# A decoder layer: the second half's self queries and keys carried through DRAM instead of being multiplied out again, and self attention entered with fewer waits

## The reference

```python
x = x + self_attn(layernorm(x))          # 16 heads of 8, causal, scale 1/sqrt(128)
    qvk = h @ Wqvk; scores = q.k per head; softmax; @ v; @ Wo
x = x + cross_attn(layernorm(x), ctx)    # 16 heads of 8, keys = ctx @ Wk + bk
    k = ctx @ Wk + bk; v = ctx @ Wv + bv; softmax(q.k * 8**-0.5) @ v; @ Wo + bo
x = x + experts(layernorm(x))            # top 2 of 8, relu(x @ W1 + b1) @ W2 + b2
```

## Time and profile before

| | us |
|---|---|
| median of 3 runs | 936.83 |
| profiled execution | 941.72 |
| its span | 940.0 |
| ScalarE busy, share of the span | 832.9, 89% |
| TensorE busy, share of the span | 865.0, 92% |
| VectorE busy, share of the span | 500.2, 53% |

### The profile page before, as it was taken

How to read it: one execution, slowest core, us unless ns; L and a number is a source line. 1 busy time by engine, 2 the same in 40 slices (tenths; PEclk the granted TensorE clock), 3 DMA queues, 4 the chain that set the end, 5 groups by cost and what they waited for, 6 DMA issues and landing times.

```text
span 940.0 us, 16020 instructions
## 1 busy us (share of the span) xinstructions
PE 865.0 (92%) x6269; PEld 273.5 (29%) x6269; DVE 500.2 (53%) x981; ACT 832.9 (89%) x694; POOL 47.5 (5%) x104
## 2 busy tenths in 40 slices
PE   6987898999889999998999998999999999999997
PEld 4562222222222222222222232222233222223543
DVE  4765653341278767867875217255635553654432
ACT  4667887999999999999999999999999999998432
POOL 4000000000000000000000004000000000001300
PEclk9996998999999999999999999999999999999999
DMA  4153003811121111121221113323123310102120
GB/s 150 71 220 66 1 1 84 271 38 39 37 37 35 35 37 38 34 55 28 46 48 38 37 35 99 82 59 57 57 60 60 57 58 23 46 23 77 36 101 14
DMA packets 24814, 56.16 MB, mean 60 GB/s; under 512 B 6986, under 2 KB 12084, under 8 KB 24476
## 3 DMA queue, kind: packets, MB, share of 16 engines
q1 hardware_dynamic: 21276, 44.18, 18.5%
q0 software_dynamic: 3456, 10.88, 3.7%
HBM read 37.59 MB, written 9.59 MB: 50 GB/s over the span
## 4 chain that ended last, share of the span: by engine, by line
PE 54%; ACT 28%; issue 13%; DVE 4%; DMA 1%; SPq 0%; ACTq 0%; DVEq 0%
ACT probs L890 28%; PE psum L1731 23%; PE psum L1695 12%; PE psum L2023 3%; PE psum L2031 3%; PE psum L1676 2%; PE psum L1550 1%; PE psum L1590 1%; PE psum L1968 1%; PE psum L1669 1%; PE psum L1594 1%; PE psum L1851 1%; DVE turned L1128 1%; PE psum L1961 1%; PE psum L1727 1%
## 5 line engine op out<-in xcount | busy, mean ns | idle before, releaser
L890 ACT ACTIVATE probs<-psum 128x1536 f32<-128x1536 f32 x562 | 765.5, 1527 | 32.1 <-PE psum L1695 16.4
L1731 PE MATMUL psum<-probs,v_ctx 128*9 128x512 f32 x3080 | 402.7, 595 | 2.9 <-DVE turned L1128 2.9
L1695 PE MATMUL psum<-q_all,k_ring 32*128 32x512 f32 (+1 forms) x1732 | 284.2, 491 | 51.3 <-ACT probs L890 46.1
L1695 PEld LDWEIGHTS psum<-q_all,k_ring 32*128 32x128 f32 x1732 | 109.8, 185 | 403.6 <-ACT probs L890 356.8
L1171 DVE TENSOR_SCALAR attnT<-psum 128x512 f32<-128x512 f32 x60 | 41.5, 692 | 127.7 <-PE psum L1669 125.9
L1731 PEld LDWEIGHTS psum<-probs,v_ctx 128*9 128x9 f32 x3080 | 45.9, 88 | 98.8 <-issue 93.0
L961 ACT ACTIVATE probs<-psum,b_sb 128x512 f32<-128x512 f32 x32 | 22.0, 687 | 34.0 <-PE psum L2023 33.4
L1128 DVE STREAM_TRANSPOSE turned<-psum 128x512 f32<-128x512 f32 x16 | 11.5, 717 | 75.2 <-PE psum L1727 57.1
L1731 PE MATMUL psum<-probs,v_self 128*9 128x512 f32 (+3 forms) x384 | 43.0, 549 | 2.1 <-DVE probs L1149 1.4
L1182 DVE SCALAR_TENSOR_TENSOR kparts_bc<-kparts_bc,attnT 128x512 f32<-128x512 f32 x60 | 41.5, 692 | 2.0
L1172 DVE SCALAR_TENSOR_TENSOR attnT<-attnT,psum 128x512 f32<-128x512 f32 x60 | 41.2, 687 | 2.0
(11 more groups left out here) (247 smaller groups left out, 631.2 us busy)
## 6 DMA issues: line engine op xcount, KB each, us to landing
k_ring<-kc_parts SPq DMA_DIRECT2D x256, 52.0 KB
k_ring<-kc_parts SPq DMA_DIRECT2D x256, 48.0 KB
kc_parts<-kparts_bc SPq DMA_DIRECT2D x8, 512.0 KB, 2.8
q_all<-w_region POOLq DMA_DIRECT2D x13, 256.0 KB, 2.6
q_all<-ctx_region POOLq DMA_DIRECT2D x13, 256.0 KB, 2.7
kc_parts<-probs SPq DMA_DIRECT2D x4, 512.0 KB, 3.0
w_region<-in_L_ffn_W SPq DMA_DIRECT2D x1, 2048.0 KB, 10.4
probs<-gate_rows SPq DMA_DIRECT2D x2, 1024.0 KB, 5.5
```

The lines of the kernel that those rows point to most:

```text
L890: act.activation(probs[:, slot:slot + w, :], psum[:, at:at + w, :], ACT.Exp, scale=SC[ph]).then_inc(L[ph]["exp_done"], 1)
L1695: mm = pe.matmul(into[:, col:col + n_q], keys, q_all[rows, g, hf * HALF + q0:hf * HALF + q0 + n_q], start=True, stop=True)
L1731: mm = pe.matmul(into[:, q0:q0 + w], v_all[:, h, t, :], probs[:, place(ph, at)[1], col:col + w], start=first, stop=last)
```

## The change

**Quads.** Only the first half of the rows still gets quad products: 8, for 4 quads times queries and keys. For the second half the plain queries and keys of `self_squares`, which are in PSUM anyway, are split by ScalarE (high) and VectorE (low) into `self_parts` (in `attnT` and `heads`, free so long). SyncE stores the four parts, 256 KB each, to DRAM behind chunk 1's store, and lays them on the quads' rows by 32 loads of 8 partitions x 4 quads x 512 columns: two behind each store of chunks 4 to 11, 16 behind the last one. TensorE waits for all 32 before group 13 (`SECOND_HALF`).

**Entry.** `kparts` is turned, so that the last chunk is not in `probs`; the banks of the context's keys change places (`kctx_bank`), so that banks 0 to 2 are free earlier. ScalarE and VectorE read the verdict inside the chunk loop; the four copies of the cross query weights are made in chunk 8 rather than behind chunk 12. TensorE scores group 0 before the last norms and before its waits for the last chunk. ScalarE's waits for the squares to be read and for the one ring buffer in `probs` now stand ahead of group 2. VectorE clears the sums' bank between its reductions rather than behind them.

The core of the diff:

```diff
+def kctx_bank(c):
+    return 3 - c % 2
...
-        kparts = [kparts_a, kparts_bc[:, 0], kparts_bc[:, 1]]
+        kparts = [kparts_bc[:, 0], kparts_a, kparts_bc[:, 1]]
+        self_parts = ((attnT[:, 0:HALF], attnT[:, HALF:2 * HALF]), [heads[:, n * HALF // 32:(n + 1) * HALF // 32, :, :]
+                                                                    .rearrange("p c g d -> p (c g d)") for n in range(2)])
...
+            def store_self_parts():
+                sp.wait_ge(s["qkquad_split"], 2)
+                for which in range(2):
+                    for part in range(PARTS):
+                        sp.dma_start(qk_dram[which, part], self_parts[which][part]).then_inc(s["qk_stored"], 16)
+            def load_self_quads(n):
+                which, r, j = n // 16, n // 4 % 4, n % 4
+                if n == 0:
+                    sp.wait_ge(s["qk_stored"], 16 * 2 * PARTS)
+                row, part = ROWS * r + HD * j, (j // 2 if which else j % 2)
+                sp.dma_start((q_all, k_self)[which][row:row + HD, :, HALF:2 * HALF].bitcast(F32),
+                             qk_dram[which, part].rearrange("(g r d) c -> r d g c", g=QUADS, r=LANES)[r])\
+                    .then_inc(s["qk_loaded"], 16)
+            loaded = 0
             for c in range(NCHUNK):
                 w = min(CHUNK * P, KV - c * CHUNK * P)
                 sp.wait_ge(s["kctx_split"], c + 1)
                 sp.dma_start(kc_dram.rearrange("i p c -> p i c")[:, :, c * CHUNK * P:c * CHUNK * P + w],
                              kparts[c % KRING][:, :, 0:w]).then_inc(s[f"kctx_stored{c % KRING}"], 16)
+                if c == 1:
+                    store_self_parts()
+                todo = 0 if c < 4 else SELF_LOADS if c < NCHUNK - 1 else 32
+                for n in range(loaded, min(loaded + todo, 32)):
+                    load_self_quads(n)
+                loaded += todo
             for n in range(KRING):
                 sp.wait_ge(s[f"kctx_stored{n}"], 16 * len(range(n, NCHUNK, KRING)))
...
                 here = slice(n // 2 * HALF, (n // 2 + 1) * HALF)
                 act.activation((sq_q, sq_k)[n % 2][:, here], bank(QK_BANKS[n]), ACT.Square).then_inc(s["sq_self"], 1)
+                if n >= 2:
+                    evac(self_parts[n % 2][0].bitcast(F32R), bank(QK_BANKS[n]), s["qkquad_high"])
             def ctx_transposed(c):
...
-            for m in range(4 * QUADS):
+            for m in range(2 * QUADS):
                 act.wait_ge(s["qkquad_ps"], m + 1)
                 if m >= 2:
-                    act.wait_ge(s["qkquad_split"], m - 1)
+                    act.wait_ge(s["qkquad_split"], 2 + m - 1)
                 evac(high[:, m % 2, :].bitcast(F32R), bank(QK_BANKS[m % 4]), s["qkquad_high"])
...
             for c in range(1, NCHUNK):
                 ctx_keys(c)
                 if c + 2 < NCHUNK:
                     ctx_transposed(c + 2)
-            act.wait_ge(s["wlate_loaded"], 16 * LATE)
-            quad_weights(2, wq_sb[:, :], [sign * QUERY_SCALE for sign in Q_SIGNS], s["wcross_quads"])
+                if c == 6:
+                    self_bounded = verdict_of(act, 0)
+                if c == 8:
+                    act.wait_ge(s["wlate_loaded"], 16 * LATE)
+                    quad_weights(2, wq_sb[:, :], [sign * QUERY_SCALE for sign in Q_SIGNS], s["wcross_quads"])
...
+            def squares_read():
+                act.wait_ge(s["norms_done"], 2)
+                act.wait_ge(s["kctx_stored1"], 16 * len(range(1, NCHUNK, KRING)))
...
             def exponentials(ph, begin, end):
...
                     held = before_in(ph, g, 3)
+                    if ph == 0 and g == 2:
+                        squares_read()
                     if held is not None:
                         act.wait_ge(L[ph]["pv_batches"], batches_through(ph, held))
                     act.activation(probs[:, slot:slot + w, :], psum[:, at:at + w, :], ACT.Exp,
...
                             ins.then_inc(G[ph]["turned"], 1)
-            for n in range(KRING):
-                act.wait_ge(s[f"kctx_stored{n}"], 16 * len(range(n, NCHUNK, KRING)))
-            choose(act, 0, lambda: exponentials(0, 0, n_groups(0)), lambda: general_exponentials(0))
+            def general_self():
+                squares_read()
+                general_exponentials(0)
+            act.cond(self_bounded, lambda: exponentials(0, 0, n_groups(0)), general_self)
             exponentials(1, 0, PART_AT)
...
-            for m in range(4 * QUADS):
-                g, which, hf = m // 4, m // 2 % 2, m % 2
-                dve.wait_ge(s["qkquad_high"], m + 1)
-                dst = (q_all, k_self)[which][:, g, hf * HALF:(hf + 1) * HALF]
+            for n in range(2, 4):
+                dve.wait_ge(s["qkquad_high"], n - 1)
+                step(dve.tensor_tensor(self_parts[n % 2][1].bitcast(F32R), bank(QK_BANKS[n]), self_parts[n % 2][0],
+                                       ALU.subtract), "qkquad_split")
+            for m in range(2 * QUADS):
+                g, which = m // 2, m % 2
+                dve.wait_ge(s["qkquad_high"], 2 + m + 1)
+                dst = (q_all, k_self)[which][:, g, 0:HALF]
                 step(dve.scalar_tensor_tensor(dst, bank(QK_BANKS[m % 4]), low[:, which:which + 1], high[:, m % 2, :],
                                               ALU.mult, ALU.subtract), "qkquad_split")
...
+                if c == 7:
+                    self_bounded = verdict_of(dve, 0)
...
-            dve.wait_ge(s["norms_ctx"], 1)
+            dve.wait_ge(s["norms_done"], 2)
+            norm_columns(bank(7), (KT + 1) * H - HALF, 2)
+            dve.memset(bank(OUT_BANK), 0.0).then_inc(s["outs_cleared"], 1)
             norm_columns(bank(6), HALF, 0)
-            norm_columns(bank(7), (KT + 1) * H - HALF, 2)
-            dve.memset(bank(OUT_BANK), 0.0).then_inc(s["outs_cleared"], 1)
...
             def query_squares(hf):
+                if hf == 0:
+                    for n in (0, 2):
+                        dve.wait_ge(s[f"kctx_stored{n}"], 16 * len(range(n, NCHUNK, KRING)))
...
             def self_quads():
-                for m in range(4 * QUADS):
-                    g, which, hf = m // 4, m // 2 % 2, m % 2
-                    if m < 4:
+                for m in range(2 * QUADS):
+                    g, which = m // 2, m % 2
+                    if m < 2:
                         pe.wait_ge(s["sq_self"], m + 1)
+                    elif m < 4:
+                        pe.wait_ge(s["qkquad_split"], m - 1)
                     else:
-                        pe.wait_ge(s["qkquad_split"], m - 3)
-                    pe.matmul(bank(QK_BANKS[m % 4]), quad_weight(which, g), xnT[:, hf * HALF:(hf + 1) * HALF],
+                        pe.wait_ge(s["qkquad_split"], 2 + m - 3)
+                    pe.matmul(bank(QK_BANKS[m % 4]), quad_weight(which, g), xnT[:, 0:HALF],
                               start=True, stop=True).then_inc(s["qkquad_ps"], 1)
...
+            def last_norms():
+                norms_of_ctx(range((NCHUNK - 2) * CHUNK, KT + 1), NCHUNK).then_inc(s["norms_done"], 1)
...
             def score_group(ph, group):
                 first, w, psum_at, _ = GROUPS[ph][group]
+                if ph == 0 and group == SECOND_HALF:
+                    pe.wait_ge(s["qk_loaded"], 16 * 32)
...
-            pe.wait_ge(s["consts_made"], N_CONSTS)
-            pe.wait_ge(s["kctx_split"], NCHUNK)
-            pe.wait_ge(s["vctx_done"], NCHUNK)
-            pe.wait_ge(s["tail_done"], 1)
-            pe.wait_ge(s["vself_done"], 2)
+            def context_read():
+                pe.wait_ge(s["kctx_split"], NCHUNK)
+                pe.wait_ge(s["vctx_done"], NCHUNK)
+                pe.wait_ge(s["tail_done"], 1)
...
             def self_attention():
-                for group in range(2):
-                    score_group(0, group)
+                pe.wait_ge(s["kctx_split"], NCHUNK - 1)
+                score_group(0, 0)
+                last_norms()
+                context_read()
+                score_group(0, 1)
                 attention(0, first_half, 0, n_groups(0))
```

38 lines of the change are left out of this document (22 added, 16 removed).

## The result

| | kernel before | changed kernel |
|---|---|---|
| median of the timed runs | 937.18 us (4 runs, 936.36 to 940.20) | 927.73 us (4 runs, 926.11 to 928.11) |
| profiled execution, its span | 941.72, 940.0 | 927.39, 925.7 |
| ratio, with its 95% interval | | 0.9875 (0.9854 to 0.9897) |

The change makes the kernel 9.5 us faster by these medians, 11.7 by the ratio; 927.0 was forecast. The profiles alone would say 14.3: the profiled execution of before, 941.72, was longer than all four of its timed runs. To see what belongs to the change, I went through the chain from point to point. In all views of the changed kernel the lines have moved: L1550, L1577, L1555, L1695, L1731, L890 are L1613, L1640, L1618, L1762, L1798, L941 now.

The account below looks back on a forecast made before the run. The two attention phases' exponentials, sums and scores were taken to set the end; the change shortens the 70 us ahead. Terms -6.9 - 3.0 + 0.3 - 0.3 = -9.9 us, from the 936.8 median: 927, range 922.5 to 931.

Parts of the forecast that it names:

- The quads, -6.9: Quad products ahead of the chunk loop: TensorE issues 8 instead of 16 at 0.86 us each, -6.9 us, bounds -6.3 and -6.9.
- The loads in the loop, +0.3: Context chunk loop: added stores and loads on the DMA engines cost +0.3 us, bounds 0 and +2.6.
- The case of loads on one half of the engines: Chunk loop: that half is asked for 2.67 us per chunk of 2.38; after eight chunks stores land some 2.4 us later.
- The stall of 0.7 us: Chunk loop: stores landing 2.4 us later, less 1.7 us to spare in the three ring buffers, leave a 0.7 us stall.
- The packets' rival (961): Self-parts loads: packets, not bytes, price them; at 2.1 us a load 34 us are lost, 961; chance 0.04 (slower).
- p = 1.35: Price in us of one self-parts load at which the whole gain of 9.9 us would be eaten.
- The hand-over, -3.0: Entry to self attention: first exponential starts at 65.75 instead of 68.79, -3.0 us, bounds -3.8 and -1.6.
- VectorE's lateness, nothing or a few tenths: Start of self attention: first mask waits until 2 us after exponential 0, caught up three masks later; costs nothing or a few tenths.
- The clock, -0.3, bounds -5 and +2: Exponentials 0 to 14: TensorE's clock falls once more, 1 to 2 us later against the groups; -0.3 us, bounds -5 and +2.
- the 25 to 29: Distance in us from the first exponential to exponential 14; leaving this range would mean the prediction is wrong.
- it falls once more: Early self attention: TensorE's granted clock falls one more time; part of the forecast case, 927, chance 0.66.
- it stays up: Rival for early self attention: clock does not fall, 3.9 us gained in place of 0.3, 923.4; chance 0.12.

Follow-up runs that it names:

- the kernel that still waits for the store: Kernel before with only the 8 quad products replaced by stores and loads through DRAM, hand-over as before: 935.16 us (12 runs), ratio 0.9948.
- the third profile: Profile from the third measurement of the changed kernel, unaltered, beside the kernel before: 929.33 us (8 runs) against 941.40, ratio 0.9898.

## Why the prediction was right

927.0 was forecast and 927.73 measured, by the steps that were named: the products gone and the hand-over shortened, -10.3 us by the rows beside a forecast of -9.9. That the two times agree to 0.7 us is luck, since single executions of this kernel spread over 10 us.

- **The quads, -6.9:** -6.87, from the same two pieces of the chain. The added evacuations and subtractions do not show, so the bound of -6.3 was not needed.
- **The loads in the loop, +0.3:** 0; the loop is 28.81 us in both. The price of one load was taken as 0.66 us from the k_ring row. It is 0.44 in the changed kernel and 0.84 in a row of 32, so 0.66 was between the two. The case of loads on one half of the engines is nearer to the spacing of 4.55 us with eight loads. By the Trainium skill (DMA: Bandwidth & Descriptors, Why a DMA increments its semaphore by 16 and not by 1) a load of 8 rows goes to the 8 lowest engines; the share of 0.53 to 0.55 in these windows agrees, though it could as well be all engines for half of the time. The stall of 0.7 us that I worked out from it did not come. By the estimate with 0.44 us, two loads and a store ask for 2.24 us of a chunk's 2.38; the stores landed 1.1 us later than before, within the 1.7 us of slack. What did not hold is that issuing a pair of loads fits beside every store: ahead of the last one it did not, and held it up by 0.7 us.
- **The packets' rival (961) and its point p = 1.35:** ruled out, but nearer than I thought. With all the loads at the end, 0.84 us each were enough to lose 7 to 9 us. The point was also summed up wrongly: with 16p - 10.2 the gain of 9.9 is eaten at p = 1.26, and the terms give 9.9 (eight chunks with 1.02 us free and 1.7 of slack) where 10.2 stands.
- **The hand-over, -3.0:** -3.45. The step was right and a size was off: TensorE's branch was put at 0.4 to 0.5 us, like ScalarE's, and cost at most 0.2. That the loads delay the last store I had left out of this part; it costs 1.9 us, but only in the kernel that still waits for the store.
- **VectorE's lateness, nothing or a few tenths:** the first mask came 2.3 us after the end of exponential 0, 2 forecast; the sums came 5.14 us after its start, against 4.95 forecast. To move the reductions gained nothing that could be measured.
- **The clock, -0.3, bounds -5 and +2:** the changed kernel's three profiles have -1.1, +0.9 and -2.6 us against the one of before. The term is a draw, within its bounds, and 24.61 us lies outside the 25 to 29 that I had given as a sign of being wrong, though the kernel was the same; the cases "it falls once more" and "it stays up" both happened, in different executions. I had given them 0.66 and 0.12 as though one of them belonged to the kernel. The Trainium skill (TensorE: Matmul & The Clock Gate, HAM oscillation) tells of a kernel that waits for a DMA between short busy stretches, and whose clock falls again each time. TensorE's waits here are for ScalarE and VectorE, 1.63 us at most from 65 to 84 in the third profile, and there the clock stayed at 1.00 from 72 to 84: "each time" did not carry over to this kernel.
- **The scale:** I subtracted from the median of the runs, 936.8, and not from the profiled execution, 941.7. The profile's own difference is 14.3 us, and would have misled by 4. The median of before then came out at 937.2 in these runs.

## What to carry to other kernels

When a product only repeats what already exists on other partitions, its place can be taken by DMA if the transfers are spread over a stretch with idle engines and enough are done before the wait. At one or two a chunk the 32 loads replaced 6.9 us of products for nothing, as long as nobody waited for the store beside them; the same loads made the kernel 7 to 9 us slower than that when all came last, and 9 to 11 when they came eight at a time. Don't carry the duration of a small load from one place to another without a factor of two on either side. And compare two executions by the stretches of their chains and at the same granted clock, before a difference in the last per cent is put down to an edit.

## What the runs showed that I had not expected

- Loads from DRAM into 8 partitions move 77 to 204 GB/s at nearly one and the same DMA share, 0.48 to 0.55 (windows of 4 us). The rate goes more with the kernel than with the execution. For the self loads behind the loop: 77 to 100 with 32 of them, 104 to 141 with 24 (three profiles), 149 to 164 with 16 in five profiles, 175 to 201 in two more. For the k_ring loads behind them: 90 to 122 in the kernel before and in that with the hand-over alone, 82 to 96 with eight loads a chunk, 121 to 126 with none, 167 to 186 with one, 160 to 204 with two. What sets it was not isolated: loads in the loop alone do not make the later ones fast, as the kernel with eight shows.
- A small DMA can hold up a large one in two ways. The last store was issued 0.7 us late, because its queue was still issuing two loads, and landed after 3.9 us instead of 2.7. Loads issued behind it account for about 0.6 us of that, by one profile with 32 behind and none ahead (3.3 us).
- Executions of one kernel differ by up to 10 us here (925.9 to 935.8), and their mean granted clocks by 0.9 points in 100; the longer ones are those with the lower clock. Two profiles show where: 3.6 us in exponentials 0 to 14, and some 6 us in one place of cross attention.
